# A two-layer gated transformer on one core: the router moved into attention layer 1, FFN normalisation into its second layer, a value projection split

## The chip, the cores and the metric

One core of a Trainium2 chip runs the whole program. The metric is the device time of one execution in microseconds; lower is better. An execution is the span that the profiler sees plus a little around it.

## What is computed

Cut to what matters (B=32 sequences, S=112 rows, D=256, 375 context rows, 16 heads of 16):

```
x = x + tanh(g_xattn[0]) * attention0(layernorm(x), ctx, mask0)
x = x + tanh(g_ffn[0])   * ffn0(layernorm(x))            # three +-1 weight matrices, 1024 wide
x = x + tanh(g_xattn[1]) * attention1(layernorm(x), ctx, mask1)
xf = layernorm(x)                                        # 3584 rows ("tokens")
probs = softmax(xf @ Wr)                                 # 8 experts
e = argmax(probs); rank = how many earlier tokens chose e; keep = rank < 448
y[token] = p[token] * relu(xf[token] @ W1[e]) @ W2[e]    for kept tokens
x = x + tanh(g_ffn[1]) * y
```

## The kernel before

Five engines run their own instruction lists and meet at semaphores. The phases run one after another, each in a block of its own: setup, queries 0, attention 0, FFN, queries 1, attention 1, logits, ranks, experts. Between two phases all engines meet and the semaphores of the old one are cleared.

`attention_phase` (L532) handles one sequence a step, software-pipelined and written out: in step s, `s.back(n)` is the sequence n steps older. Keys are made for s-1 (p), row maxima for s-3 (x), scores, exponentials and the weighted sum for s-4 (d), and the head outputs are turned, normalised, projected and added to the residual for s-5 (e). TensorE's `body` interleaves by hand 12 score units, 14 row scores, two key products, the value products (L770), the turns of e's heads (L833, L840), the projection (L856) and the weighted sum (L825). VectorE reduces each row score (L1030, "row") from a ring of three PSUM banks, splits keys (`low_keys`, L1069), normalises heads, and makes `low_heads` (L1061), which raises `back_ready`. ScalarE takes the exponentials (L952) and copies out of PSUM. GpSimd masks 8 of the 12 units (L699) and makes the low part of the context (L707). SyncE issues all loads and stores; `x_sum` (two buffers) is loaded at L674 and stored to DRAM at L681. After step 36 the phase ends.

`logits_phase` then reloads the rows from DRAM four sequences at a time, normalises them (with a square root on ScalarE), turns them and multiplies by Wr. `ranks_phase` is one chain of small VectorE instructions that makes expert, rank, slot and probability of every token. In `experts_phase` SyncE issues expert 0's weights (L1690, L1691), then waits for `put`, that is, for all 32 indirect DMAs (L1725) with which GpSimd scatters the rows to `expert_in`, and only then loads expert 0's rows. ScalarE and VectorE split the weights into high and low halves (L1784, L1824), TensorE turns the rows (L1740) and runs the products (L1757, L1771).

`ffn_phase` (L1112) takes four sequences a step. Its products are numbered z = 0 to 15: 0 to 7 are the first layer (4 matmuls each), 8 to 15 the second (16 each). VectorE makes the low half of each (L1233) and, for the next group, runs statistics after z=4 and the normalisation after z=6; TensorE turns those rows after z=11. Mask work stands at z=8, 9, 10, 14, 15.

## Time and profile before

| | |
|---|---|
| median of 3 runs | 1799.13 us (1794.83 to 1804.24) |
| profiled execution | 1798.14 us, of it span 1796.4 us |
| TensorE / VectorE / ScalarE / GpSimd busy | 84% / 62% / 45% / 47% |
| attention 1, last residual add to the experts' first product | 122.3 us |
| mean granted TensorE clock | 0.918 |

Busy shares are means over phases with different limits; the 122.3 us are from 1496.2 to 1618.46 in the profile. A clock of 1.00 is 2.4 GHz, 0.50 is 1.2 GHz.

### The profile page before, as it was taken

Reading aid. Unit: us, or ns where it says so; the run is one execution under the profiler, and the core shown is the slowest. Engines: PE = TensorE matmul, PEld = TensorE weight load, DVE = VectorE, ACT = ScalarE, POOL = GpSimd, SP = SyncE. Lnnn points to the kernel's source line nnn. Section 1 sums busy time; section 2 is a strip of 40 time slices with the busy share of each in tenths; the row PEclk is TensorE's granted clock in tenths of the full one; section 3 lists DMA queues with packets and bytes.
Section 4 is the critical chain, followed back from the end, with each engine's and each line's share of the span. In section 5 each row is a group of like instructions: output and inputs, shape, how many; then the busy total and the mean of one; then the engine's idle time right before and its main releaser. Section 6 shows DMA issues by size and latency. Waiting matters only on the chain. (4 is left out here: it accounts for less than half of the span.)

```text
span 1796.4 us, 41156 instructions
## 1 busy us (share of the span) xinstructions
PE 1502.7 (84%) x15399; PEld 1094.7 (61%) x15399; DVE 1113.2 (62%) x3561; ACT 802.7 (45%) x1822; POOL 846.8 (47%) x794
## 2 busy tenths in 40 slices
PE   1739999999996899999957379999999995509996
PEld 0417777777774466555634157777777774507775
DVE  4738788787783555555537267777777774515663
ACT  3316666666663222222203146666666652114441
POOL 1247787787774000000012447777777761064332
PEclk9869999999998899999978589999999996559998
DMA  7654455455431122221136545666566522035440
GB/s 230 217 107 97 97 112 104 98 115 101 97 80 34 42 64 69 83 69 58 33 87 206 106 103 122 125 119 114 113 122 125 108 47 69 26 120 171 135 148 18
DMA packets 225380, 183.65 MB, mean 102 GB/s; under 512 B 70314, under 2 KB 218735, under 8 KB 225192
## 3 DMA queue, kind: packets, MB, share of 16 engines
q1 hardware_dynamic: 219560, 171.36, 40.9%
q0 software_dynamic: 5632, 9.78, 1.7%
q8 instruction: 118, 1.93, 0.5%
q14 instruction: 70, 0.57, 0.1%
HBM read 99.53 MB, written 48.49 MB: 82 GB/s over the span
## 5 line engine op out<-in xcount | busy, mean ns | idle before, releaser
L952 ACT ACTIVATE probs_a<-bank 125x448 f32<-125x448 f32 x768 | 388.0, 541 | 32.9 <-PE bank L809 16.6
L699 POOL TENSOR_TENSOR probs_a<-probs_a,keep_a 125x448 int32<-125x448 int32 x256 | 285.3, 1137 | 121.4 <-ACT probs_a L952 121.3
L699 POOL TENSOR_TENSOR probs_a<-probs_a,mask_keep 125x448 int32<-125x448 int32 x256 | 285.3, 1137 | 99.2 <-ACT probs_a L952 99.0
L1030 DVE CUSTOM_DVE_ANT_0 masked_scores_a<-bank,mask_add_a 112x375 bf16<-112x375 f32 x512 | 260.7, 545 | 97.4 <-PE bank L780 93.6
L1030 DVE CUSTOM_DVE_ANT_0 masked_scores_a<-bank,mask_add 112x375 bf16<-112x375 f32 x512 | 260.3, 545 | 71.0 <-PE bank L780 67.4
L780 PE MATMUL bank<-k_stack_a,q_stack_a 96*128 96x375 f16 x1024 | 292.7, 327 | 8.1 <-DMA k_stack_a<-k_low_a 3.1
L809 PE MATMUL bank<-q_stack_a,k_stack_a 97*128 97x224 f16 x1536 | 253.1, 259 | 16.9 <-DMA q_stack_a<-max_t_a 16.1
L809 PEld LDWEIGHTS bank<-q_stack_a,k_stack_a 97*128 97x128 f16 x1536 | 146.0, 98 | 78.1 <-DMA q_stack_a<-max_t_a 18.0
L1354 PE MATMUL bank<-h0h_f,ffn_w 128*128 128x448 f16 x512 | 180.6, 353 | 11.6 <-DVE h0l_f L1233 11.4
L1354 PE MATMUL bank<-h0l_f,ffn_w 128*128 128x448 f16 x512 | 180.4, 352 | 0.0
L1193 POOL DMA_DIRECT2D x_after_ffn<-y_f x8 | 5.9, 743 | 346.1 <-DVE y_f L1240 346.1
L825 PE MATMUL bank<-probs_a,values_a 125*32 125x112 f32 x6144 | 161.7, 260 | 2.7 <-POOL probs_a L699 2.4
L825 PEld LDWEIGHTS bank<-probs_a,values_a 125*32 125x32 f32 x6144 | 144.8, 110 | 23.4 <-issue 19.3
L707 POOL TENSOR_TENSOR ctx_low_a<-ctx_in_a,ctx_high_a 128x375 f16<-128x375 f32 x128 | 113.0, 903 | 70.0 <-ACT ctx_high_a L930 70.0
L749 PE MATMUL bank<-ctx_high_a,wk_high 128*128 128x375 f16 x256 | 87.4, 341 | 51.5 <-POOL ctx_low_a L707 46.8
L975 ACT ACTIVATE heads_t_a<-bank 128x448 f32<-128x448 f32 x64 | 34.8, 544 | 204.5 <-PE bank L825 204.5
L780 PEld LDWEIGHTS bank<-k_stack_a,q_stack_a 96*128 96x128 f16 x1024 | 99.7, 98 | 43.4 <-DVE row_max_a L1030 10.9
L1305 ACT ACTIVATE h1h_f<-bank 128x448 f16<-128x448 f32 x64 | 34.8, 544 | 167.0 <-PE bank L1354 167.0
L1233 DVE SCALAR_TENSOR_TENSOR h1l_f<-bank,h1h_f 128x448 f16<-128x448 f32 x64 | 40.0, 625 | 111.0 <-ACT h1h_f L1305 111.0
L770 PE MATMUL bank<-wv_high,ctx_high_a 128*128 128x256 f16 x384 | 104.8, 273 | 1.7 <-DVE k_low_a L1069 1.6
L770 PE MATMUL bank<-wv_high,ctx_low_a 128*128 128x256 f16 x384 | 104.6, 272 | 0.0
L770 PE MATMUL bank<-wv_low,ctx_high_a 128*128 128x256 f16 x384 | 104.4, 272 | 0.0
(208 smaller groups left out, 3208.7 us busy)
## 6 DMA issues: line engine op xcount, KB each, us to landing
k_stack_a<-k_high_a SPq DMA_DIRECT2D x256, 96.0 KB, 4.1
ctx_in_a<-in_ctx_dram SPq DMA_DIRECT2D x64, 375.0 KB, 3.6
w_in_e<-in_L_ffn_W_dram SPq DMA_DIRECT2D x16, 1024.0 KB
k_stack_a<-k_low_a SPq DMA_DIRECT2D x128, 96.0 KB, 4.2
q_stack_a<-q_split SPq DMA_DIRECT2D x128, 84.0 KB, 3.4
x_and_bias<-xb_q SPq DMA_DIRECT2D x16, 448.0 KB, 4.5
q_split<-high_q SPq DMA_DIRECT2D x32, 224.0 KB, 3.7
x_sum_a<-x_and_bias SPq DMA_DIRECT2D x64, 112.0 KB, 4.2
```

The lines of the kernel that those rows point to most:

```text
L699: pool.tensor_tensor(bits, bits, cols, ALU.mult).then_inc(masked, 1)
L707: pool.tensor_tensor(ctx_low[s.four][:, cols], ctx_in[s.two][:, c, :], ctx_high[s.four][:, cols], ALU.subtract).then_inc(ctx_low_ready, 1)
L749: last = pe.matmul(work_bank[:, 0:S2], w[:, c, j * P:(j + 1) * P], part[p.four][:, c * S2:(c + 1) * S2], start=c == 0 and n == 0, stop=c = ...
L770: last = pe.matmul(work_bank[:, (k % 2) * D:(k % 2 + 1) * D], part[x.four][:, at:at + P], w[:, c, :], start=c == 0 and n == 0, stop=c == K ...
L780: pe.matmul(bank_of(x, h)[:, 0:S2], q_stack[x.four][0:STACK, at:at + P], k_stack[x.four][0:STACK, (h // 2) * WIDE:(h // 2) * WIDE + S2], s ...
L809: last = pe.matmul(bank[:, half * 2 * S:(half + 1) * 2 * S], k_stack[d.four][0:ROWS, at:at + P], q_stack[d.four][0:ROWS, (2 * t + half) * ...
L825: last = pe.matmul(head_bank[QUAD * j:QUAD * (j + 1), t * S:(t + 1) * S], values[d.two][:, k, 4 * t + j, :], probs[:, i, j * S:(j + 1) * S ...
L952: act.activation(probs[:, i, :], score_bank[i % 3][0:CK, 0:GT], ACT.Exp, scale=DK ** -0.5).then_inc(exped, 1)
L975: act.activation(heads_t[:, :], head_bank[:, 0:GT], ACT.Copy).then_inc(heads_ready, 1)
L1030: dve.tensor_tensor_reduce(masked_scores[:, use_of[x.value, h] % 3, :], bank_of(x, h)[0:S, 0:S2], mask_add[x.four][:, 0:S2], 1.0, -LARGEST ...
L1233: dve.scalar_tensor_tensor(out=low[:, j, :], in0=z_bank[z % 4][:, 0:GT], scalar=0.0, in1=high[:, j, :], op0=ALU.max, op1=ALU.subtract).the ...
L1354: last = pe.matmul(z_bank[z % 4][:, 0:GT], w[layer][:, c, j * P:(j + 1) * P], part[:, c, :], start=c == 0 and n == 0, stop=c == chunks - 1 ...
```

## The change

Logits and ranks phases go. Attention 1 gets their work, later in the pipeline: VectorE measures row f = s-6, GpSimd takes its power -0.5, ScalarE normalises row s-7 into `sent_rows`, TensorE turns it and in the next step multiplies it by Wr (`route_products`); four sequences together choose, count, order and place in the steps 12 to 15 behind their first, one or no small VectorE instruction in each of four slots of a step, and GpSimd scatters sequence s-16. The phase runs 48 steps in place of 37 (`LAG`). `x_sum` has four buffers. `make_values(0, 1)` is split in two calls in both layers. In the FFN, statistics move from z=4 to z=9, the end of normalisation from 6 to 11, the turn from 11 to 12, the low rows from 12 to 13, the mask's turn from 13 to 14.

```diff
-        attention_phase(nc, m, 1, based, out, a["ctx_1024"], (add_1, keep_1), q_split)
-        moe_phases(nc, m, a, expert_in, out)
+        attention_phase(nc, m, 1, based, out, a["ctx_1024"], (add_1, keep_1), q_split, (a["L1_ffn_Wr"], expert_in))
+        experts_phase(nc, m, a, expert_in, out)
...
-        x_sum = many(2, sb, "x_sum", [S, D], F32)
+        x_sum = many(4, sb, "x_sum", [S, D], F32)
...
+        LAG = 16 if layer else 5
...
-                    wait(sp, x_stored[d.two], 16 * d.use2)
-                    sp.dma_start(x_sum[d.two][:, :], take(x_in, d.value)).then_inc(x_loaded[d.two], 16)
+                    wait(sp, x_stored[d.four], 16 * d.use4)
+                    if layer:
+                        wait(sp, xn_ready, d.value - 3)
+                    sp.dma_start(x_sum[d.four][:, :], take(x_in, d.value)).then_inc(x_loaded[d.four], 16)
...
+            if layer:
+                sp.dma_start(wr[:, :, :], router.rearrange("(c p) e -> p c e", p=P)).then_inc(wr_loaded, 16)
...
-            run_quads(B, 5, body)
-            for n in range(2):
-                sp.wait_ge(x_stored[n], 16 * B // 2)
+            run_quads(B, LAG, body)
+            for n in range(4):
+                sp.wait_ge(x_stored[n], 16 * B // 4)
...
+            def take_root(f):
+                pool.wait_ge(measured, 4 * f.value + 3)
+                wait(pool, xn_ready, f.value)
+                pool.tensor_tensor(root[:, :], spread[:, :], half[:, :], ALU.pow).then_inc(rooted, 1)
+            def number_tokens(quad):
+                pool.wait_ge(routed, routed_at(quad, "shifted"))
+                slots = slice(G * (quad % 3), G * (quad % 3) + G)
...
+            def send_rows(w):
+                pool.wait_ge(routed, routed_at(w.quad, "put"))
+                pool.wait_ge(numbered, w.quad + 1)
...
+                at = G * (w.quad % 3) + w.four
+                pool.indirect_dma_start(expert_in[:, :],
+                                        bass.IndirectOffsetOnAxis(put[w.quad % 3][:, w.four:w.four + 1], 0),
+                                        sent_rows[:, at, :], None, bounds_check=E * CAP - 1,
+                                        oob_is_err=False).then_inc(sent[at], 16)
...
+                f = s.back(6)
                 for i in pool_units:
+                    if i == pool_units[5] and layer and f.exists(B):
+                        take_root(f)
...
+                if layer:
+                    t, w = s.back(14), s.back(16)
+                    if t.exists(B) and t.four == 0:
+                        number_tokens(t.quad)
+                    if w.exists(B):
+                        send_rows(w)
+            run_quads(B, LAG, body)
+            if layer:
+                for n in range(3 * G):
+                    pool.wait_ge(sent[n], 16 * len(range(n, B, 3 * G)))
...
-                elif p.exists(B):
+                elif ks[0] == 2 and p.exists(B):
                     pe.wait_ge(k_low_ready, KC * (p.value + 1))
-                else:
+                elif ks[0] == 2:
...
-                last.then_inc(v_made, 1)
+                if ks[-1] > 0:
+                    last.then_inc(v_made, 1)
+            def route_products(s, e):
+                f, r, t = s.back(7), s.back(8), s.back(12)
+                counts = t.exists(B) and t.four == 1
+                if not (f.exists(B) or r.exists(B) or counts):
+                    return
+                pe.wait_ge(back_ready, min(e.value + 1, B))
+                wait(pe, routes_kept, routes(s.value) - 1)
+                if r.exists(B):
+                    if r.value == 0:
+                        pe.wait_ge(wr_loaded, 16)
+                    for c in range(KC):
+                        last = pe.matmul(head_bank[0:S, 256:256 + E], xt[r.two][:, c, :], wr[:, c, :],
+                                         start=c == 0, stop=c == KC - 1)
...
+                    dst = head_bank[0:S, 288:288 + G * E].rearrange("s (b e) -> s b e", b=G)
+                    pe.matmul(dst, before[:, :], chosen[:, :, :], start=True, stop=False, skip_group_check=True)
+                    for b in range(1, G):
+                        pe.matmul(dst[:, b:, :], ones[:, :], chosen[:, b - 1, :].unsqueeze(1).to_broadcast([S, G - b, E]),
+                                  start=False, stop=False, skip_group_check=True)
+                    last = pe.matmul(dst, ones[:, :], carried[:, :].unsqueeze(1).to_broadcast([S, G, E]),
+                                     start=False, stop=True, skip_group_check=True)
+                if f.exists(B):
+                    pe.wait_ge(xn_ready, f.value + 1)
+                    for c in range(KC):
+                        last = pe.transpose(head_bank[:, c * S:(c + 1) * S],
+                                            sent_rows[:, f.value % (3 * G), c * P:(c + 1) * P], ident[0:S, 0:S])
+                last.then_inc(routes_made, 1)
...
+                if layer:
+                    wait(pe, routes_kept, routes(d.value + 4))
...
-                    make_values(x, p, e, (0, 1))
+                    make_values(x, p, e, (0,))
+                if layer:
+                    route_products(s, e)
+                if x.exists(B):
+                    make_values(x, p, e, (1,))
...
+            def normalise_rows(f):
+                act.wait_ge(measured, 4 * (f.value + 1))
+                wait(act, sent[f.value % (3 * G)], 16 * (f.value // (3 * G)))
+                act.activation(sent_rows[:, f.value % (3 * G), 0:D], x_sum[f.four][:, :], ACT.Identity,
+                               bias=shift[:, 0:1], scale=root[:, 0:1]).then_inc(xn_ready, 1)
+            def power_up(quad):
+                act.wait_ge(routed, routed_at(quad, "shifted"))
...
+                act.activation(power[:, :, :], shifted[:, :, :], ACT.Exp).then_inc(powered, 1)
+            def keep_routes(s):
+                f, r, t = s.back(7), s.back(8), s.back(12)
+                counts = t.exists(B) and t.four == 1
+                if not (f.exists(B) or r.exists(B) or counts):
+                    return
+                act.wait_ge(routes_made, routes(s.value))
+                if r.exists(B):
+                    last = act.activation(logits[r.quad % 2][:, r.four, :], head_bank[0:S, 256:256 + E], ACT.Copy)
+                if counts:
+                    last = act.activation(ranks[:, :, :].rearrange("s b e -> s (b e)"), head_bank[0:S, 288:288 + G * E],
+                                          ACT.Copy)
+                if f.exists(B):
+                    last = act.activation(xt[f.two][:, :, :], head_bank[:, 0:KC * S].rearrange("p (c t) -> p c t", c=KC),
+                                          ACT.Copy)
+                last.then_inc(routes_kept, 1)
...
+                if layer and f.exists(B):
+                    normalise_rows(f)
+                if layer and t.exists(B) and t.four == 1:
+                    power_up(t.quad)
...
                 units(9)
+                if layer:
+                    keep_routes(s)
                 if x.exists(B):
                     copy_values(x, e, (0, 1))
...
+            def measure(f, part):
+                if part == 0:
+                    dve.wait_ge(summed, f.value + 1)
+                    dve.bn_stats(stats[:, :], x_sum[f.four][:, :]).then_inc(measured, 1)
+                    return
+                if part == 1:
+                    dve.wait_ge(measured, 4 * f.value + 1)
+                    dve.bn_aggr(mean_var[:, :], stats[:, :]).then_inc(measured, 1)
+                if part == 2:
+                    dve.wait_ge(measured, 4 * f.value + 2)
+                    wait(dve, rooted, f.value)
+                    dve.tensor_scalar(spread[:, :], mean_var[:, 1:2], EPS, None, ALU.add).then_inc(measured, 1)
+                if part == 3:
+                    dve.wait_ge(rooted, f.value + 1)
+                    wait(dve, xn_ready, f.value)
+                    dve.tensor_scalar(shift[:, :], mean_var[:, 0:1], root[:, 0:1], -1.0, ALU.mult,
+                                      ALU.mult).then_inc(measured, 1)
+            def wide(table):
+                return table[:, :].unsqueeze(2).to_broadcast([S, G, E])
+            def choose(quad, part):
+                if part == 0:
+                    dve.wait_ge(routes_kept, routes(G * quad + 11))
+                    dve.tensor_reduce(top[:, :], logits[quad % 2][:, :, :], AX.X, ALU.max).then_inc(routed, 1)
+                if part == 1:
+                    dve.wait_ge(routed, routed_at(quad, "top"))
+                    wait(dve, powered, quad)
+                    dve.tensor_tensor(shifted[:, :, :], logits[quad % 2][:, :, :], wide(top), ALU.subtract).then_inc(routed, 1)
+                if part == 2:
+                    dve.wait_ge(routed, routed_at(quad, "shifted"))
+                    dve.scalar_tensor_tensor(out=marked[:, :, :], in0=shifted[:, :, :], scalar=0.0, in1=number[:, :, :],
+                                             op0=ALU.is_equal, op1=ALU.mult).then_inc(routed, 1)
+                if part == 3:
+                    dve.wait_ge(routed, routed_at(quad, "marked"))
+                    dve.tensor_reduce(first[:, :], marked[:, :, :], AX.X, ALU.min).then_inc(routed, 1)
+            def count(quad, part):
+                if part == 0:
+                    dve.wait_ge(routed, routed_at(quad, "first"))
+                    wait(dve, routes_made, routes(G * quad + 9) if quad else 0)
+                    dve.tensor_tensor(chosen[:, :, :], number[:, :, :], wide(first), ALU.is_equal).then_inc(routed, 1)
...
+            def order(quad, part):
+                if part == 0:
+                    dve.wait_ge(routed, routed_at(quad, "inverse"))
+                    slots = slice(G * (quad % 3), G * (quad % 3) + G)
+                    dve.tensor_scalar(sent_rows[:, slots, D], chance[:, :], m["gate"][0:S, 3:4], W_SCALE ** -2,
+                                      ALU.mult, ALU.mult).then_inc(routed, 1)
+                if part == 1:
+                    dve.wait_ge(routes_kept, routes(G * quad + 13))
+                    dve.tensor_tensor(carried[:, :], carried[:, :], counted[:, :], ALU.add).then_inc(routed, 1)
+                if part == 2:
+                    dve.tensor_tensor(picked[:, :, :], ranks[:, :, :], chosen[:, :, :], ALU.mult).then_inc(routed, 1)
...
+            def place_rows(quad, part):
+                if part == 0:
+                    dve.wait_ge(routed, routed_at(quad, "rank"))
+                    dve.tensor_scalar(over[:, :], rank[:, :], float(CAP), float(2 * E * CAP), ALU.is_ge,
+                                      ALU.mult).then_inc(routed, 1)
...
+            def route(t, part):
+                if layer and t.exists(B):
+                    (choose, count, order, place_rows)[t.four](t.quad, part)
...
+                rows(2)
+                if layer and o.exists(B):
+                    measure(o, 3)
+                rows(3)
+                rows_measured(0)
                 if p.exists(B):
                     low_keys(p, 0)
-                rows(4, 5, 6, 7)
+                rows(4)
+                rows_measured(1)
+                rows(5)
+                rows_measured(2)
+                rows(6, 7)
                 if p.exists(B):
                     low_keys(p, 1)
                 if e.exists(B):
                     normalise(e)
                 if x.exists(B):
                     shift_parts(x, 0)
-                rows(8, 9, 10)
+                rows(8)
+                route(t, 0)
+                rows(9)
+                route(t, 1)
+                rows(10)
+                route(t, 2)
                 if e.exists(B):
                     low_heads(e)
-                rows(11, 12)
+                rows(11)
+                route(t, 3)
...
-                        if z == 4:
+                        if z == 9:
                             normalise(s)
-                        if z == 6:
+                        if z == 11:
                             normalise_end(s)
-                        if z == 12:
+                        if z == 13:
...
-                        if z == 5:
+                        if z == 10:
                             act.wait_ge(var_ready, s.value + 1)
                             act.activation(dev[:, :], mean_var[:, :, 1], ACT.Sqrt, bias=m["eps"][0:S, :]).then_inc(dev_ready, 1)
-                        if z == 12:
+                        if z == 13:
                             for c in range(KC):
...
-                    if s.exists(NG) and z == 11:
+                    if s.exists(NG) and z == 12:
                         turn(s)
-                    if p.exists(NG) and z == 13:
+                    if p.exists(NG) and z == 14:
                         turn_mask(s, p)
                 if p.exists(NG):
...
-def moe_phases(nc, m, a, expert_in, out):
...
-def logits_phase(nc, m, a, x_in, route):
...
-def ranks_phase(nc, m, route):
...
-def experts_phase(nc, m, a, route, expert_in, out):
+def experts_phase(nc, m, a, expert_in, out):
...
-                    if isinstance(s.value, int) and s.value == 0:
-                        sp.wait_ge(put, 16 * B)
...
-            pool.wait_ge(m["experts_cleared"], 16)
-            for b in range(B):
-                pool.indirect_dma_start(expert_in[:, :], bass.IndirectOffsetOnAxis(route["put"][:, b:b + 1], 0),
-                                        route["rows"][:, b, :], None, bounds_check=E * CAP - 1,
-                                        oob_is_err=False).then_inc(put, 16)
```

## Rows read from the trace of the kernel before

**Rows 1.** Busy time by stretch: us, PE, PEld, DVE, ACT, POOL, PEclk, DMA, GB/s.
```profile
580.00:925.00 345.00, 314.98 (x1952) 193.22 (x1952) 171.44 (x352) 78.66 (x153) 5.95 (x8) 0.97 0.21 61
...
1200.00:1350.00 150.00, 144.76 (x1940) 114.38 (x1933) 113.13 (x423) 97.48 (x236) 112.13 (x106) 1.00 0.61 118
...
1569.50:1618.50 49.00, 1.79 (x9) 1.48 (x10) 8.06 (x12) 5.36 (x10) 32.31 (x34) 0.50 0.38 127
```
**Rows 2.** Chain that ended last: start us, us, what.
```profile
1570.49 40.96 issue
...
1618.46 11.57 PE bank L1757 x48
```
**Rows 3.** Timeline around the last two phases (start us, us, engine, line).
```profile
1495.77 0.43 DVE L1055 SCALAR_TENSOR_TENSOR x_sum_a<-bank,x_sum_a 112x256 f32<-112x256 f32 x1 [1.62 <-PE bank L856]
...
1501.96 0.40 SPq L1438 DMA_DIRECT2D wr_l<-in_L_ffn_Wr_dram  x1
...
1566.77 0.18 DVE L1619 TENSOR_SCALAR base_k<-first_k 112x32 f32<-112x32 f32 x1
...
1569.59 0.38 SPq L1690 DMA_DIRECT2D w_in_e<-in_L_ffn_W_dram  x1
...
1578.75 4.27 ACT L1784 ACTIVATE w_high_e<-w_in_e 128x512 f16<-128x512 f32 x8 [21.00 <-DMA w_in_e<-in_L_ffn_W_dram]
1579.41 4.99 DVE L1824 SCALAR_TENSOR_TENSOR w_low_e<-w_in_e,w_high_e 128x512 f16<-128x512 f32 x8 [7.54 <-issue]
```
**Rows 4.** Timeline, GpSimd: the last of the 32 scatters.
```profile
1609.25 0.94 POOL L1725 DMA_INDIRECT expert_in<-rows_r,put_r  x1 [0.30 <-issue]
```
**Rows 5.** TensorE's waits in the FFN (total us, times, longest).
```profile
PE bank L1354 <- DVE h0l_f L1233: 11.4, 9, 1.6
```
**Rows 6.** Timeline, VectorE, one FFN group.
```profile
680.54 1.41 DVE L1204 BATCH_NORM_STATS2 stats_f<-xg_f 112x6 f32<-112x256 f32 x4
682.09 0.38 DVE L1208 BATCH_NORM_AGGREGATE mean_var_f<-stats_f 112x2 f32<-112x6 f32 x4
...
684.01 1.38 DVE L1218 TENSOR_SCALAR xn_f<-xg_f,mean_var_f,scale_f 112x256 f32<-112x256 f32 x4
```
**Rows 7.** Timeline, TensorE, one step of attention 1.
```profile
1293.38 0.36 PE L840 MATMUL bank<-ident,heads_q_a 112*128 112x112 f32 x2
...
1294.58 0.27 PE L770 MATMUL bank<-wv_high,ctx_high_a 128*128 128x256 f16 x1
...
1295.24 0.32 PE L780 MATMUL bank<-k_stack_a,q_stack_a 96*128 96x375 f16 x1
```
**Rows 8.** Timeline, VectorE, the same step.
```profile
1288.76 0.55 DVE L1069 SCALAR_TENSOR_TENSOR k_low_a<-bank,k_high_a 128x375 f16<-128x375 f32 x1
...
1294.40 0.39 DVE L1061 TENSOR_TENSOR heads_low_a<-bank,heads_high_a 128x224 f16<-128x224 f32 x1 [0.23 <-ACT heads_high_a L996]
```
**Rows 9.** Timeline, GpSimd, the same step and the start of the next.
```profile
1292.80 3.32 POOL L699 TENSOR_TENSOR probs_a<-probs_a,keep_a 125x448 int32<-125x448 int32 x3 [0.30 <-ACT probs_a L952]
...
1297.64 1.76 POOL L707 TENSOR_TENSOR ctx_low_a<-ctx_in_a,ctx_high_a 128x375 f16<-128x375 f32 x2
1301.54 1.13 POOL L699 TENSOR_TENSOR probs_a<-probs_a,keep_a 125x448 int32<-125x448 int32 x1 [2.14 <-ACT probs_a L952]
```
**Rows 10.** Timeline: VectorE instructions beside GpSimd ones, two places.
```profile
930.41 4.63 POOL L351 TENSOR_TENSOR xb_q<-xg_q,bo 112x1024 f32<-112x1024 f32 x2 [11.06 <-DMA xg_q<-x_after_ffn]
...
932.77 2.29 DVE L383 TENSOR_TENSOR scale_q<-scale_q,seen 112x4 f32<-112x4 f32 x1
...
1469.12 7.71 POOL L699 TENSOR_TENSOR probs_a<-probs_a,keep_a 125x448 int32<-125x448 int32 x7 [3.69 <-ACT probs_a L952]
...
1472.43 1.14 DVE L1039 TENSOR_SCALAR max_parts_a<-row_max_a 112x8 f16<-112x8 f32 x1
```
**Rows 11.** Timeline: TensorE loads of the logits phase, and table loads of ScalarE.
```profile
1513.79 3.06 PEld L1460 LDWEIGHTS bank<-wr_l,xt_l 128*112 128x112 f32 x16 [1.77 <-ACT xt_l L1487]
...
1042.38 1.28 ACT L952 ACT_TABLE_LOAD   x1
```

296 lines of the change are left out of this document (86 added, 210 removed).

## The prediction

> **What bounds the kernel now.** I read the busy time by stretch first. In attention 1 TensorE is busy 144.76 of 150 us at full clock, and in the FFN 314.98 of 345 [rows 1]: there it sets the pace, and whatever is added to its list, or stalls it, costs time. VectorE and GpSimd are each at 112 to 113 of 150 us in attention 1, so they have 3.3 us idle in a step of about 13.5. Between the last residual add and the experts TensorE does little: from 1569.5 to 1618.5 it is busy 1.79 of 49 us, at clock 0.50 [rows 1]. The chain of waits says why: 40.96 us in which SyncE waits for the scatters, then a load, and the first expert product at 1618.46 [rows 2]. The timeline gives the other end: the last residual add ends at 1495.77 + 0.43 = 1496.20 [rows 3]. So 122.3 us lie between attention and experts, and that is what most of the change is about.
>
> **The stretch behind attention, after.** Five terms.
> (a) From the last add to GpSimd's root: statistics 0.35 (a quarter of 1.41 [rows 6]), their aggregate 0.1 (0.38 / 4), one small instruction 0.2 [rows 3], then the power. No row shows a power on GpSimd; I take 0.5, between 0.2 (a small VectorE instruction) and 2.35 (half of 4.63, GpSimd's 1024-wide addition [rows 10]). With the hops 1.5.
> (b) GpSimd's list then holds 11 scatters (sequences 21 to 31, one a step, in the steps 37 to 47). One takes 0.94 + 0.30 idle = 1.24 [rows 4]: 13.7. The chain that places the last four sequences (turn, logits, copy, some 15 small VectorE instructions of 0.2, the count products) is 8 to 9 us and runs beside the first seven scatters (8.7), so it sets nothing, or 1 us.
> (c) The last scatter's landing: before, the last one ended at 1609.25 + 0.94 = 1610.19 and SyncE went on at 1570.49 + 40.96 = 1611.45 [rows 2, 4]: 1.3.
> (d) Ending the block: before, 1496.20 to 1501.96 [rows 3] is 5.8 with the store of the last rows in it, which I estimate at half; 2.8 is left, and 26 more semaphores to clear, an estimated 0.04 each, make it 3.8.
> (e) From the experts' first weight load to their first product: no scatter is waited for, and rows of expert 0 are issued right behind its weights. Then the weight split is last: it ended at 1579.41 + 4.99 = 1584.40, 14.8 behind the load's issue at 1569.59 [rows 3]. The two low row halves of about 0.6 each come behind it: 16.1, against 48.9 before.
> Sum: 1.5 + 13.7 + 1.3 + 3.8 + 16.1 = 36.4. The stretch shrinks by 122.3 - 36.4 = **85.9 us**. The bounds are narrow, 80 to 89. If the rows of expert 0 queued behind expert 1's weights, they would land some 9 us later (the first weights landed at 1578.75, 9.2 behind their issue [rows 3]); the row load is issued ahead of them, so I don't count it.
>
> **FFN.** TensorE waited 11.4 us for the low halves of the first layer [rows 5]: statistics (1.41 + 0.38) and normalisation (1.38) stand between products of four matmuls [rows 6]. Behind z=9 and z=11 they stand between products of sixteen, 3 us each, where VectorE has only 0.6 us of its own besides the mask. The 11.4 go. What is late next: z=8 to 10 now carry mask work of 0.9 to 1.9 us and the statistics, so the normalised rows are ready about 0.25 us after TensorE asks for them behind z=12, in 7 groups: 1.8 back. Gain **9.6 us** (bounds 5 and 11.4).
>
> **Projection split.** In layer 0 the two calls follow each other with nothing between and no new wait; nothing. In layer 1 it only makes room for `route_products`, costed below. Four `x_sum` buffers: SyncE's new wait for the normalised row asks for one of the step before, already there; behind it in SyncE's queue are the key stores and the row maxima's DMA, which would pay if it were late. Router weights and small constants at the start: **1 us** (0 to 2).
>
> **The router inside attention 1.** This is the price. Per step, TensorE gets two fp32 turns and two logit products. At 1.2 GHz a pass took 3.06 / 16 = 0.19 [rows 11], so 0.1 at full clock: 0.4, and 0.45 with a quarter of the five count products. ScalarE gets an identity and two copies, about 0.9, and GpSimd a scatter of 1.24 behind the context work, where it has 2.14 us idle before the next step's first mask [rows 9], and the root. Neither should be late.
> VectorE decides. `route_products` waits for `low_heads` of the same step, before needed only by the projection, 1.8 us later. In the step shown, the value products of `make_values(0)` end at 1294.58 [rows 7], and `low_heads` ran 1294.40 to 1294.75, having waited 0.23 for ScalarE [rows 8]. Ahead of it VectorE now does statistics 0.35, aggregate 0.1 and two tiny ones 0.1 each overlapped; from step 12 three more small ones, 0.3. Without anything else `low_heads` ends at 1294.75 + 0.8 = 1295.55: TensorE stalls 1.0 and works 0.45, so 1.45 a step (1.15 without the three).
> But there is the second thing that the rows show. A VectorE instruction with two SBUF inputs, normally 0.16, took 2.29 when it began beside a GpSimd instruction and ended with it (932.77 + 2.29 = 935.06 against 930.41 + 4.63 = 935.04); a tiny SBUF-to-SBUF scalar instruction took 1.14, one GpSimd unit, at 1472.43 [rows 10]. Of the new small instructions, nine in four steps are of these kinds (two in choose, one in count, three in order, three in place). GpSimd is busy without a break from 1292.80 to 1296.12 [rows 9], just where their slots lie (behind rows 8, 9 and 10). Each can wait for the end of a unit of 1.1 us. Going through the step by hand, with GpSimd's units 0.3 later, `low_heads` ends near 1297.1 in choose, order and place and near 1295.8 in count; with the maxima's scalar instruction sometimes caught too, a step costs 3.0 on average, and 1.65 in the steps without them. Some will find a gap. I take 2.6, nearer the locked end since the rows show the lock twice, and 1.3 for the others. Steps 12 to 34 are 23: 59.8. Steps 7 to 11: 6.5. Draining steps: 2. Sum **68.3 us**; bounds 14 (TensorE's 0.45 in 30 steps alone) and 91 (3.4 each).
> The Trainium skill, SBUF — State Buffer, "SBUF: two separate sides", calls this an exclusive lock: VectorE in a two-port mode or with two SBUF inputs against GpSimd, the loser blocked for the whole instruction. By that rule, applied to every one of the nine, the price is the 80 of the locked case; by an average port share it would be the 41 of the free one. It speaks against the change.
> No table load is counted: attention 1 has its own at 1042.38, 1.28 us [rows 11], and copies stand between the exponentials without one, but no row has an identity beside them. The Trainium skill, ScalarE: Activation LUTs, "Table sets: the hidden batching unit", says that identity is in every set; no row here shows it for this one.
>
> **Sum.** 1798.14 - 85.9 - 9.6 + 1 + 68.3 = 1771.9 for the profiled execution, which lies 1.0 below the median of the runs: **1773 us**.
>
> **Rivals.**
> R1, VectorE's new work slips into its 3.3 us of idle time. For it: the idle time; GpSimd's units move too when TensorE is late. Against: the slots lie in its busiest part. At 1.45 and 1.15 a step the cost is 33 + 6 + 2 = 41, less where turns overlap, 35: 1740.
> R2, the lock bites everywhere: 80 us, 1784; with GpSimd's scatter also holding the small ones, 91, 1796.
> R3, slower: the root on GpSimd. Its list then sets the step: root, three units, context, scatter, mask. After the scatter it has 0.9 us before unit 0, and about 1.5 till its context work is needed. From a root of 2.7 us on, the change gains nothing beyond what is measurable; at 3.5 it costs 2.0 in 30 steps on top, 60: 1833. For it: no row has its price. Against: 1024 elements take 2.35.
> R4, identity and exponential change tables: two loads of 1.28 in 31 steps, 79: 1852. Against: the copies.
> R5, the change doesn't do what it says: the stall in the FFN only moves to the turn behind z=12, 9.6 back: 1782; inside my range.
>
> **How the numbers follow.** Forecast 0.50 (1752 to 1784), R1 0.25, R2 0.12, R3 0.06, R4 0.02, R5 0.05. The range, 1738 to 1797, takes in R1's centre and R2 and leaves out R3, R4 and the better half of R1. About 0.5%, 9 us, is what a measurement can tell from no change. Faster by more: forecast, R1, R5 and half of R2 and a little less, 0.86; same, the rest of R2, 0.06; slower 0.08.
>
> **What would show it.** Right: experts' first load some 20 us behind the last residual add, their first product 16 later; L1354's wait for VectorE gone; in attention 1 a wait of TensorE at the turns or logit products of 1 to 2.5 us a step, ended by `low_heads`; tiny VectorE instructions of 0.5 to 1.1 us ending with GpSimd units. Wrong: steps under 14.5 us (R1), GpSimd without idle time and TensorE waiting for masks or context (R3), table loads between exponentials (R4), or a wait elsewhere, as for the first key product behind the statistics placed ahead of `low_keys` (about 0.25 a step in my sum).

## The result, and the profile after

The changed kernel takes **1809.7 us** (median of 8 runs, 1804.75 to 1813.52) against 1799.47 of the kernel before on the same chip: ratio 1.0059, 95% interval 1.0039 to 1.0079. I forecast 1773 in a range of 1738 to 1797, so the change loses a little where I expected it to win. Its profiled execution spans 1811.9 us, against 1796.4 before. Where the 15.5 us between the spans lie, from the residual adds and the first expert product in both traces:

| stretch | before | after | difference | forecast |
|---|---|---|---|---|
| up to the first residual add of attention 1 | 1073.72 | 1061.77 | -12.0 | -8.6 |
| attention 1, first to last residual add | 422.1 | 534.8 | **+112.7** | +68.3 |
| end of the last add to the first expert product | 122.3 | 39.4 | -82.9 | -85.9 |
| the experts, first product to the end | 177.9 | 175.5 | -2.4 | 0 |

So both gains came, and the price in attention 1 is what I got wrong, by 44 us. The busy time by stretch (us, PE, PEld, DVE, ACT, POOL, PEclk, DMA, GB/s) answers to [rows 1]:
```profile
1200.00:1350.00 150.00, 131.32 (x1522) 99.87 (x1520) 109.03 (x376) 80.43 (x202) 95.35 (x96) 0.88 0.47 93
1350.00:1500.00 150.00, 130.12 (x1548) 99.69 (x1549) 111.75 (x391) 81.64 (x208) 97.28 (x98) 0.91 0.47 93
1500.00:1560.00 60.00, 53.09 (x676) 40.60 (x674) 42.44 (x153) 29.25 (x74) 36.81 (x37) 0.87 0.30 53
```
TensorE now idles 19 of 150 us where it idled 5, and the granted clock, which was 1.00 all through this stretch, is 0.88 and 0.91. No other engine has become full: in the first of these rows VectorE and GpSimd are less busy than before (109.03 and 95.35 us against 113.13 and 112.13). TensorE's longest list of waits (us in total, times, longest) has a new first line, and the FFN's line of [rows 5] is gone:
```profile
PE bank L863 <- DVE heads_low_a L1306: 57.1, 26, 3.2
...
PE bank L1753 <- DMA xg_e<-expert_in: 26.5, 1, 26.5
PE bank L1593 <- DVE xn_f L1486: 17.4, 2, 17.2
```
The timeline of one choose step (start us, us, engine, line, idle before) shows what is behind it:
```profile
1310.99 0.57 POOL L741 TENSOR_TENSOR root_a<-spread_a,half_a 112x1 f32<-112x1 f32 x1
...
1311.47 2.32 DVE L1214 SCALAR_TENSOR_TENSOR marked_a<-shifted_a,number_a 112x32 f32<-112x32 f32 x1
1311.54 2.20 POOL L736 TENSOR_TENSOR probs_a<-probs_a,keep_a 125x448 int32<-125x448 int32 x2
1313.72 0.38 DVE L1306 TENSOR_TENSOR heads_low_a<-bank,heads_high_a 128x224 f16<-128x224 f32 x1
...
1314.15 0.92 PE L863 MATMUL bank<-wr_a,xt_a 128*112 128x8 f32 x4 [2.52 <-DVE heads_low_a L1306]
```
`marked`, the third of the step's small VectorE instructions and the second that GpSimd holds up, begins 0.09 before GpSimd's root ends (1310.99 + 0.57 = 1311.56) and ends at 1313.79, just when both mask units behind the root have ended (1313.74). It works 0.19 us when nothing is in its way (run `e2_slots_first` below), so it waited through two units, not one. `heads_low` stands behind it, and TensorE stands 2.5 us at the logit products. What then happens to the clock, in stretches of 1.7 us:
```profile
1309.60:1311.30 1.70, 1.70 (x17) 1.41 (x15) 1.70 (x8) 1.70 (x6) 1.41 (x2) 1.00 0.82 170
1311.30:1313.00 1.70, 0.33 (x4) 0.05 (x1) 1.70 (x3) 0.39 (x1) 1.70 (x3) 1.00 1.15 127
1313.00:1314.70 1.70, 0.55 (x3) 0.55 (x4) 1.66 (x5) 0.00 (x0) 0.74 (x1) 0.74 0.68 85
1314.70:1316.40 1.70, 1.70 (x10) 1.36 (x11) 0.00 (x0) 0.42 (x2) 0.00 (x0) 0.50 0.30 50
...
1319.80:1321.50 1.70, 1.70 (x30) 1.07 (x32) 1.22 (x4) 0.00 (x0) 1.53 (x3) 0.75 0.02 5
```
TensorE is busy 0.88 of 3.4 us, and the clock falls from 2.4 to 1.2 GHz until about 1320.6; the products run at half speed for nearly 7 us, a loss of some 3.4 us on top of the wait. The wait comes back in each choose, order and place step, 17 times with 2.3 us or more, and the low clock stands behind 15 of the 17, for 88.7 us in all. From the residual adds most of these steps take 19 to 21 us, count steps 16, and the steps of the kernel before mostly 13.5 to 14.5. Two of the waits, 3.02 and 2.51 us, have no low clock behind them (the row from 1356 to 1392 has 1.00), and their steps took 17.5 and 17.0 us:
```profile
1356.00:1392.00 36.00, 30.46 (x448) 23.97 (x448) 29.56 (x102) 19.78 (x50) 24.97 (x26) 1.00 0.46 101
```
So in this trace the low clock makes such a step some 2.7 us longer than the wait alone.

### The profile page after: what moved, and what is told of

It reads as the page before. It is cut to its first block and busy times, and to the rows that moved or that the text cites. A ratio compares the mean times of both kernels' runs of the same rounds, so it can differ in the third digit from the quotient of the medians.

```text
span 1811.9 us, 41668 instructions
## 1 busy us (share of the span) xinstructions
PE 1534.3 (85%) x15435; PEld 1104.4 (61%) x15435; DVE 1155.5 (64%) x3677; ACT 821.2 (45%) x1907; POOL 865.4 (48%) x824
## 5 line engine op out<-in xcount | busy, mean ns | idle before, releaser
L1275 DVE CUSTOM_DVE_ANT_0 masked_scores_a<-bank,mask_add_a 112x375 bf16<-112x375 f32 x512 | 266.2, 542 | 132.8 <-PE bank L887 132.7
L887 PE MATMUL bank<-k_stack_a,q_stack_a 96*128 96x375 f16 x1024 | 304.1, 339 | 6.6 <-DVE row_max_a L1275 2.9
L916 PE MATMUL bank<-q_stack_a,k_stack_a 97*128 97x224 f16 x1536 | 259.6, 264 | 6.0 <-DMA q_stack_a<-max_t_a 5.1
L916 PEld LDWEIGHTS bank<-q_stack_a,k_stack_a 97*128 97x128 f16 x1536 | 149.7, 100 | 69.4 <-issue 6.6
L887 PEld LDWEIGHTS bank<-k_stack_a,q_stack_a 96*128 96x128 f16 x1024 | 103.5, 102 | 44.1 <-DVE row_max_a L1275 11.4
L846 PE MATMUL bank<-wv_high,ctx_high_a 128*128 128x256 f16 x384 | 108.8, 283 | 1.7 <-DVE k_low_a L1314 1.6
L846 PE MATMUL bank<-wv_high,ctx_low_a 128*128 128x256 f16 x384 | 108.8, 283 | 0.0
L846 PE MATMUL bank<-wv_low,ctx_high_a 128*128 128x256 f16 x384 | 108.5, 283 | 0.0
```

The source lines that it names most:

```text
L846: last = pe.matmul(work_bank[:, (k % 2) * D:(k % 2 + 1) * D], part[x.four][:, at:at + P], w[:, c, :], start=c == 0 and n == 0, stop=c == K ...
L887: pe.matmul(bank_of(x, h)[:, 0:S2], q_stack[x.four][0:STACK, at:at + P], k_stack[x.four][0:STACK, (h // 2) * WIDE:(h // 2) * WIDE + S2], s ...
L916: last = pe.matmul(bank[:, half * 2 * S:(half + 1) * 2 * S], k_stack[d.four][0:ROWS, at:at + P], q_stack[d.four][0:ROWS, (2 * t + half) * ...
L1275: dve.tensor_tensor_reduce(masked_scores[:, use_of[x.value, h] % 3, :], bank_of(x, h)[0:S, 0:S2], mask_add[x.four][:, 0:S2], 1.0, -LARGEST ...
```

## The experiments

In each run the kernel before ran on the same chip; ratios are to it, with the 95% interval. "Attention 1" is the time from the first to the last residual add (422.1 before, 534.8 after).

**`e1_late_products`: the router's products just ahead of the projection** (my first theory was that all that counts is TensorE's early wait for `low_heads`).
```diff
                     make_values(x, p, e, (0,))
-                if layer:
-                    route_products(s, e)
...
                 rows(13)
+                if layer:
+                    route_products(s, e)
                 if e.exists(B):
```
(ScalarE's `keep_routes` moves to the step's end with it.)

> The changed kernel with the router's products on TensorE moved from between the two value products to just ahead of the projection, and ScalarE's copies of them to the end of its step; VectorE's list is untouched, so its small instructions still stand beside GpSimd's units. Theory A (low_heads comes late because small VectorE instructions wait for GpSimd, and the early wait for it stalls TensorE, after which its clock falls): the wait of 57 us falls to under 20, the granted clock in attention 1 goes back above 0.97, and the time falls by 60 to 80 us to about 1740. Theory B (VectorE simply has too much work in the step, wherever TensorE waits): the wait only moves to the projection and to the row banks, the time falls by less than 20 us, to 1790 or more.

Measured: 1843.3 us, ratio 1.0251 (1.0226 to 1.0277); attention 1 took 567.2. A miss of 100 us, and the timeline tells how (one place step):
```profile
1297.11 0.57 POOL L741 TENSOR_TENSOR root_a<-spread_a,half_a 112x1 f32<-112x1 f32 x1
...
1297.56 5.12 DVE L1260 SCALAR_TENSOR_TENSOR place_a<-first_a,rank_a 112x4 f32<-112x4 f32 x1
1297.66 3.30 POOL L736 TENSOR_TENSOR probs_a<-probs_a,keep_a 125x448 int32<-125x448 int32 x3
1300.93 1.73 POOL L766 TENSOR_TENSOR ctx_low_a<-ctx_in_a,ctx_high_a 128x375 f16<-128x375 f32 x2
```
GpSimd's work now follows the root without a gap: five instructions, three mask units and two of the context, and `place` ends with the last of them (1302.68 against 1302.66). Of the wait at the logit products (L863) 1.3 us were left, and TensorE stood at the row scores (L887) and at the turn of the row maxima (L896) instead, up to 4.7 us at a time:
```profile
PE bank L887 <- DVE row_max_a L1275: 48.1, 20, 4.5
PE bank L896 <- DVE row_max_a L1275: 34.2, 22, 4.7
```
This points at VectorE's instruction, wherever TensorE meets it; e2 and e14 below test it.

**`e2_slots_first` and `e3_both`: the first three VectorE slots at the step's start.** The latter has e1's late products too.
```diff
+                route(t, 0)
+                route(t, 1)
+                if t.four != 1:
+                    route(t, 2)
                 rows(2)
...
-                rows(8)
-                route(t, 0)
-                rows(9)
-                route(t, 1)
-                rows(10)
-                route(t, 2)
+                rows(8, 9, 10)
+                if t.four == 1:
+                    route(t, 2)
```

> The changed kernel with the router's small VectorE instructions of slots 0, 1 and 2 moved from behind rows 8, 9 and 10 to the start of the step, ahead of row 2, where VectorE waits for TensorE and GpSimd has few units (the third slot of the counting step stays, as it needs the powers of the same step). The products stay where the change has them. Theory A (the lock with GpSimd is what delays low_heads): the instructions shrink from 0.5 to 2.3 us to about 0.2, a step costs about 1.5 us over before as in the unlocked case, and the time is 1745 to 1765, the upper end if the clock still falls. Theory B (amount of work on VectorE): the same instructions cost the same in total, the time stays above 1790.

> Both moves together. Theory A: nothing waits for low_heads any more, TensorE has only its added 0.45 us a step, the clock stays at 1.00: attention 1 costs 14 to 25 us over before, the time is 1715 to 1730. Theory B: above 1780.

Measured: e2 1727.8 us, ratio 0.9612 (0.9587 to 0.9637), attention 1 450.8, better than expected; e3 1719.5 us, ratio 0.9551 (0.9524 to 0.9578), 445.1, as expected. The same instructions, in e2, by line (count | busy us, mean ns), and its wait at the logit products:
```profile
L1214 DVE SCALAR_TENSOR_TENSOR marked_a<-shifted_a,number_a 112x32 f32<-112x32 f32 x8 | 1.5, 193 | 0.3
...
L1260 DVE SCALAR_TENSOR_TENSOR place_a<-first_a,rank_a 112x4 f32<-112x4 f32 x8 | 1.2, 151 | 0.0
```
```profile
PE bank L863 <- DVE heads_low_a L1306: 3.5, 10, 1.0
```
0.19 and 0.15 us instead of 2.3, 3.5 us of waiting instead of 57, and the clock is 1.00 again. The late products, beside which e1 got slower, bring another 0.6% here.

**`e4_ffn_alone`: the kernel before with only the FFN's new places** (`normalise` at z=9 instead of 4, its end at 11 instead of 6, and what follows from them).
```diff
-                        if z == 4:
+                        if z == 9:
                             normalise(s)
...
-                        if z == 6:
+                        if z == 11:
                             normalise_end(s)
```

> The kernel before with the FFN's part of the change alone (statistics behind z=9, normalisation behind 11, turn behind 12, low rows behind 13, mask's turn behind 14). As predicted: 9.6 us faster than before, so about 1789. Rival (the stall moves to the turn): within 2 us of before.

Measured: 1785.1 us, ratio 0.9914 (0.9885 to 0.9942). The traces say 12.1 us: the load that starts attention 1's queries lies at 913.70 instead of 925.75. TensorE's wait for `h0l_f`, 11.4 us, is gone and none came in its place. From the last residual add of attention 0 to that load, which leaves out what came before, it is 338.1 us instead of 351.8, so 13.6 less (11.1 less in the changed kernel).

**`e5_fill_stall`: the changed kernel, TensorE kept working in the stall.** 24 useless products ahead of the wait for `low_heads`, in steps 12 to 34 but for count.
```diff
+            wv_fill = m["wv"][layer][0]
...
+                if 12 <= s.value < 35 and t.four != 1:
+                    for _ in range(24):
+                        pe.matmul(work_bank[:, 256:448], wv_fill[:, 0, 0:P], wv_fill[:, 1, 0:192], start=True, stop=True, skip_group_check=True)
                 pe.wait_ge(back_ready, min(e.value + 1, B))
```

> The changed kernel with 24 useless f16 matmuls of 192 columns (0.08 us each at full clock, 1.9 us) on TensorE just ahead of its wait for low_heads, in steps 12 to 34 except the counting ones, where it otherwise stands idle for 2.5 to 3.2 us. Nothing else is changed, so VectorE's waits for GpSimd stay. Theory C (a part of the loss is TensorE's clock, which falls to half behind each such stall): the half-clock stretches in attention 1, 88 us in the changed kernel, fall to under 30, and the time falls by 20 to 40 us, to 1770 to 1790. Theory D (the clock is a by-product; VectorE's list alone sets the step): the time stays within 8 us of 1810.

Measured: 1777.3 us, ratio 0.9888 (0.9857 to 0.9918), 32 us less than the changed kernel (31 by the ratios) for more work; attention 1 498.0, 36.8 less. By stretch, the clock is back:
```profile
1200.00:1350.00 150.00, 140.88 (x1847) 111.32 (x1839) 122.53 (x421) 84.52 (x223) 106.05 (x108) 1.00 0.53 104
```
VectorE's instructions are untouched (`marked` still takes 2.3 us), and the useless products take up part of the wait (25.0 us of it are left) without ending it sooner. Of the 88.7 us at the low clock, 3.4 are left. So the run parts the two: the low clock after the stall costs some 32 to 37 of the 112.7 us.

**`e6_early_wait`: the kernel before with only the split and the early wait.**
```diff
-                last.then_inc(v_made, 1)
+                if ks[-1] > 0:
+                    last.then_inc(v_made, 1)
...
                 if x.exists(B):
-                    make_values(x, p, e, (0, 1))
+                    make_values(x, p, e, (0,))
+                if layer and e.exists(B):
+                    pe.wait_ge(back_ready, e.value + 1)
+                if x.exists(B):
+                    make_values(x, p, e, (1,))
```

> The kernel before with the projection split and, between its halves in attention 1, only the wait for low_heads of the same step, without any router work. By the rows of before TensorE gets there at 1294.58 and low_heads ends at 1294.75, so 0.2 us a step, some 5 us: 1800 to 1808. If the early wait by itself were the cause (its place, not what delays low_heads), it would cost over 20 us.

Measured: 1801.7 us, ratio 1.0021 (1.0006 to 1.0036): about 4 us, as expected. The wait asked 1.8 us earlier is nearly free by itself: what counts is what delays `low_heads`.

**`e7_small_two_source` and `e9_small_one_source`: the kernel before with three useless small VectorE instructions** behind rows 8, 9 and 10 in steps 12 to 35, an addition of two [112 x 32] tiles in e7, of one tile and a constant in e9.
```diff
+            def small(s, n):
+                if layer and 12 <= s.value < 36:
+                    dve.tensor_tensor(scr[n][:, :], scr_a[:, :], scr_b[:, :], ALU.add).then_inc(small_done, 1)
...
-                rows(8, 9, 10)
+                rows(8)
+                small(s, 0)
+                rows(9)
+                small(s, 1)
+                rows(10)
+                small(s, 2)
```

> The kernel before with one useless VectorE addition of two [112, 32] SBUF tensors behind each of the rows 8, 9 and 10 in steps 12 to 35 of attention 1 (72 instructions of 0.19 us); no router, no early wait. Theory W (an instruction with two SBUF inputs waits until GpSimd has nothing ready, so for its whole run of units): single instructions of 3 to 5 us, 2 to 4 us a step and more where the clock follows, the time is 1850 to 1930. Theory U (it waits for the one unit that runs, as I predicted): none above 1.15 us, the time is 1805 to 1835.

> The same as e7 with instructions of one SBUF input (the same tensor plus a constant). If the wait for one unit belongs to this kind, as the maxima's scalar instruction of 1.14 us in before suggests, none is above 1.15 us and the time is 1805 to 1835, well under e7. If the kind makes no difference, it equals e7.

Measured: 1817.4 us, ratio 1.0111 (1.0081 to 1.0141), and 1816.2 us, 1.0115 (1.0083 to 1.0147). 72 instructions take 756 and 757 ns in the mean and none over 1.18 us, so one source or two is the same. In e7's timeline:
```profile
1300.24 3.32 POOL L701 TENSOR_TENSOR probs_a<-probs_a,keep_a 125x448 int32<-125x448 int32 x3 [0.30 <-ACT probs_a L954]
1300.60 0.83 DVE L1042 TENSOR_TENSOR scr_a<-scr_a_a,scr_b_a 112x32 f32<-112x32 f32 x1
1301.81 0.71 DVE L1042 TENSOR_TENSOR scr_a<-scr_a_a,scr_b_a 112x32 f32<-112x32 f32 x1
```
Three units of 1.11 us from 1300.24 end at 1301.35, 1302.45 and 1303.56; the two additions end at 1301.43 and 1302.52, each with one unit. This is what I had forecast of the lock. Most steps take 14.8 us, attention 1 takes 441.9, 19.8 more than before, and the clock stays at 1.00. The lock by single units isn't what made steps of 20 us.

**`e10_root_last`: the changed kernel, only GpSimd's root moved** from between the masks to behind the context work.
```diff
                 for i in pool_units:
-                    if i == pool_units[5] and layer and f.exists(B):
-                        take_root(f)
...
                     low_context(s, 1)
+                if layer and f.exists(B):
+                    take_root(f)
```

> The changed kernel with one thing moved: GpSimd takes its power (the root, 0.57 us) behind the context work, at the end of its step, in place of between units 6 and 7. VectorE's small instructions and TensorE's early wait stay where the change has them. In the changed kernel the long waits (2.3 us, and 5.1 with the products late) are all of a two-input instruction that arrives 0.1 us before the root ends, and last through all units behind it; the others last to the end of one unit. Theory R (the root, or an arrival beside it, is what makes the long wait): no instruction above 1.2 us, the time falls by 25 to 50 us to 1760 to 1785. Theory S (any second locked instruction in a step waits for the run): still over 2 us in each such step, the time stays within 10 us of 1810.

Measured: 1757.2 us, ratio 0.9822 (0.9791 to 0.9853); attention 1 478.7. In a choose step:
```profile
1220.12 3.32 POOL L736 TENSOR_TENSOR probs_a<-probs_a,keep_a 125x448 int32<-125x448 int32 x3 [0.67 <-ACT probs_a L1065]
1221.70 0.70 DVE L1214 SCALAR_TENSOR_TENSOR marked_a<-shifted_a,number_a 112x32 f32<-112x32 f32 x1
1222.32 0.38 DVE L1306 TENSOR_TENSOR heads_low_a<-bank,heads_high_a 128x224 f16<-128x224 f32 x1
```
```profile
PE bank L863 <- DVE heads_low_a L1306: 35.5, 26, 2.1
```
`marked` takes 0.70 instead of 2.32 and ends at 1222.40, with the second unit (1220.12 + 2.21 = 1222.33). TensorE waits 35.5 us instead of 57.1, never over 2.1, and the clock is 0.99 where it was 0.88. One instruction of 0.57 us in another place is worth 2.4%, some 42 us, within the fall that I had expected. (The two traces differ by 56.1 us in attention 1: the changed kernel's is of its slowest run, e10's of its fastest.)

**`e11_small_beside_power` and `e12_small_beside_add`: e7 and a useless [112 x 1] instruction on GpSimd at the root's place**, a power in e11, an addition in e12.
```diff
...
+                    if i == pool_units[5] and layer and 12 <= s.value < 36:
+                        pool.tensor_tensor(gp_c[:, :], gp_a[:, :], gp_b[:, :], ALU.pow).then_inc(gp_done, 1)
                     if d.exists(B):
                         mask_unit(d, i)
```

> Kernel e7 (before, with three useless two-input VectorE additions a step) and a useless power of a [112, 1] tensor on GpSimd between units 6 and 7, in steps 12 to 35. In e7 the additions waited 0.7 to 0.83 us, to the end of one unit. Theory R: the second addition, which will arrive beside the power, now lasts 2 us or more in most steps, and the time rises by over 20 us above e7's 1817. Theory S: waits stay at 0.7 to 1.1 us, the time rises by the 0.57 us at most, to under 1830.

> The same with an addition in place of the power on GpSimd, so a short instruction at the same place. If the long wait comes from the power itself, it is absent here; if from where VectorE's instruction arrives beside any short instruction ahead of a run, it may be here too, and the time is that of e11 or between e7 and e11.

Measured: e11 1889.0 us, ratio 1.0548 (1.0510 to 1.0587); e12 1866.3 us, ratio 1.0421 (1.0385 to 1.0457). So 24 instructions of 0.55 us on an engine with idle time cost 4.4% beyond e7, some 78 us, and 24 of 0.19 us cost 3.1%. First e11, then e12:
```profile
1292.32 0.55 POOL L717 TENSOR_TENSOR gp_c_a<-gp_a_a,gp_b_a 112x1 f32<-112x1 f32 x1
1292.80 2.30 DVE L1047 TENSOR_TENSOR scr_a<-scr_a_a,scr_b_a 112x32 f32<-112x32 f32 x1
1292.84 3.30 POOL L702 TENSOR_TENSOR probs_a<-probs_a,keep_a 125x448 int32<-125x448 int32 x3
```
```profile
1303.45 0.19 POOL L717 TENSOR_TENSOR gp_c_a<-gp_a_a,gp_b_a 112x1 f32<-112x1 f32 x1
1303.60 2.23 POOL L702 TENSOR_TENSOR probs_a<-probs_a,keep_a 125x448 int32<-125x448 int32 x2
1303.93 1.94 DVE L1047 TENSOR_TENSOR scr_a<-scr_a_a,scr_b_a 112x32 f32<-112x32 f32 x1
```
e11 makes the long wait from parts, in the kernel before: the addition ends at 1295.10, two units behind the power (1292.84 + 2.20 = 1295.04). A third unit and the context work follow without a gap, so here the wait ends inside the run, where in e1 it ended with it. e12 says that it isn't the power as an operation: a plain addition of 0.19 does it too, though the VectorE instruction comes 0.3 us into the unit behind it (it ends at 1305.87, with the second unit, 1305.83). The clock from 1200 to 1350 is 0.91 and 0.95 in these two and 1.00 in e7, though no stall of TensorE in e12 is long; the longest line of its waits there is
```profile
PE bank L794 <- DVE row_max_a L1039: 30.8, 23, 1.5
```

**`e14_late_root_last` and `e13_all_three`: e1 and e3, each with e10's edit.**

> e1_late_products and e10_root_last together: the router's products just ahead of the projection, GpSimd's root behind its context work, the VectorE instructions still behind rows 8, 9 and 10. Theory R (e1 lost because the second small VectorE instruction met the root and waited through five GpSimd units, 5.1 us, where in the changed kernel it was 2.3): the 5.1 us instructions are gone, none is longer than 1.2 us, steps are 15 to 16.5 us, and since the products have 2 us more room than in e10 it comes out at or below e10, 1735 to 1757. Rival L (late products are themselves what cost e1 its 34 us against the changed kernel, by holding ScalarE's or VectorE's work for the next step): it stays above e10 by 20 us or more, 1780 to 1830, with short VectorE instructions and a wait elsewhere.

> e3_both with GpSimd's root behind its context work as well. Theory R: with the first three VectorE slots at the step's start nothing small lies beside the root or the run of masks behind it any more, so moving the root brings nothing: within 5 us of e3_both, 1714 to 1725. Rival: the root in the middle of the masks costs the masks or the small instructions left behind rows 2 to 7 something still; then 1700 to 1713. If the root now comes too late for the scatter in the same step, a few us more than e3_both, 1726 to 1735.

Measured: e14 1730.4 us, ratio 0.9629 (0.9613 to 0.9645), attention 1 454.9. The one edit that parts it from e1 takes away 6.2% of the kernel before's time, some 112 us, and e1's miss is settled: late products are good, the root ahead of GpSimd's run is what hurt. TensorE's wait at the turn of the row maxima, 34.2 us and up to 4.7 at a time in e1, is small:
```profile
PE bank L896 <- DVE row_max_a L1275: 15.1, 22, 1.1
```
e13 1713.3 us, ratio 0.9530 (0.9513 to 0.9548), attention 1 433.8. That is 0.2% under e3, with intervals that overlap, so I can't say that the root still costs something there. With e3 it is the fastest version, 4.7% under the kernel before: the change's idea was sound, and its order within the step was not. Over the kernel before, attention 1 grew, in one trace of each, by 145.1 us in e1, 112.7 in the changed kernel, 76.0 in e5, 56.7 in e10, 32.8 in e14, 28.7 in e2, 23.1 in e3 and 11.7 in e13.

## Why the prediction was wrong, point by point

**The stretch behind attention: right.** Forecast 36.4, measured 39.4. The chain and the timeline, which answer to [rows 2 to 4]:
```profile
1621.41 0.40 SPq L1712
...
1621.86 7.70 DMA w_in_e<-in_L_ffn_W_dram
...
1630.24 4.90 DVE w_low_e L1837 x8
1635.14 1.07 DVE x_low_e L1862 x2
1636.22 0.14 issue
1636.35 11.77 PE bank L1770 x48
```
```profile
1596.56 0.42 DVE L1300 SCALAR_TENSOR_TENSOR x_sum_a<-bank,x_sum_a 112x256 f32<-112x256 f32 x1 [2.66 <-PE bank L965]
...
1597.94 0.57 POOL L741 TENSOR_TENSOR root_a<-spread_a,half_a 112x1 f32<-112x1 f32 x1 [4.45 <-DVE spread_a L1193]
...
1611.32 0.94 POOL L755 DMA_INDIRECT expert_in<-sent_rows_a,put_a  x1 [0.30 <-issue]
```
(a) The root ends 1.5 behind the last add (1598.51 against 1596.98), as forecast; it takes 0.57 where I took 0.5. (b) Eleven scatters end at 1612.26, 13.75 later; forecast 13.7. (c) and (d) The first load comes 9.15 behind that, where I had 5.1. The lines of the block's end say where the 4 us are (ns: shortest, median, longest; start of the first and the last):
```profile
L1376 POOLq DRAIN  x2: 2673/3455/4237, 564.5 to 1614.1; - x2
L97 SPq EVENT_SEMAPHORE_RANGE_CLEAR  x72: 25/30/35, 1617.0 to 1621.1; - x72
```
GpSimd drains for 2.67 us from 1614.11; only then do the engines meet and SyncE clears the 72 semaphores, 4.1 us. Before, the same drain began at 1486.0, beside attention's last work, and clearing 46 semaphores took 3.1 us. So the 26 more cost the 1.0 us that I had estimated; what I had at nothing is the drain, which now stands behind the last scatter, and some 1 us is the rest of (d) and the landing, which I had a little short. (e) 14.9 from the load to the first product, forecast 16.1, with the weight split last, as said. It makes up for 1.2 of the 4, by luck.

**FFN: right in kind, too low.** 12.1 to 13.6 by e4 against 9.6, above my bound of 11.4. The stall went as said; the 1.8 us that I took back at the turn didn't come, no wait is left there. What comes on top of the 11.4 us of waiting isn't traced.

**Projection split, start: nothing speaks against it.** The first residual add is 12.0 earlier, the FFN's 12.1. But kernels that don't differ up to that add (before, e7, e9, e11, e12) have it anywhere from 1067.85 to 1074.92, so the 1 us that I had for the start can't be read.

**The router in attention 1: the failed step**, 112.7 against 68.3, and above the bound of 91. The place of the wait was right (TensorE at the logit products, ended by `low_heads`), and so were the instructions that delay it and the lock that delays them. Wrong was the sentence "each can wait for the end of a unit of 1.1 us". Some waited longer: behind the root, for two units in the changed kernel (2.3 us) and five instructions in e1 (5.1 us). With the root elsewhere (e10) each waits for one unit, and attention 1 grows by 56.7 us, inside my bounds and below my 68.3. So the term was sized rightly for single units, with bounds that had no room for the run, and 56 of the 112.7 us in the traces (42 by the medians of the runs) hang on the root's place. This share and that of the clock below overlap: with the root elsewhere TensorE's wait falls by 21.6 us, and most of the low clock goes with it. I had the root in view, but only asked how long it takes (R3), not what lies behind it when it ends.

The second omission is in the sum itself, which has **no term for the clock**. [rows 1] showed 1.00 in this stretch, and I carried it over to a kernel into which I had just put a stall. Roughly, the 112.7 are 57.1 of waiting, some 40 of lost clock (0.12 x 150, 0.09 x 150, 0.13 x 60, and 3 from 1060 to 1200, at 0.98) and 14 of the work added to TensorE (my 0.45 in 31 steps); this split is an estimate, and e5 shows 32 to 37 of the 40. The Trainium skill, TensorE: Matmul & The Clock Gate, "HAM oscillation — how this bites in real kernels", describes a wait that comes back with every tile and leaves TensorE at its low clock each time; the trace agrees in the main, with 0.50 granted behind 15 of the 17 long stalls, for nearly 7 us behind eleven of them.

**Rivals.** R1 (idle time absorbs it, 35 us) is out for this order, but in e13's order the router costs less still: 11.7 us in attention 1, about TensorE's added work alone. R2 (lock everywhere) had the right side and priced a lock of one unit; 1796 was its end. (Its 91 us can't be had from 3.4 us in 23 steps: with 1.65 in five and 2 for draining that is 88.5. Nothing hangs on it.) R3: the root takes 0.57, not 2.7, and GpSimd isn't full; a slow root isn't it. R4: no table load lies between the exponentials, though an identity ran at 1308.36 between exponentials in the step shown; the Trainium skill, ScalarE: Activation LUTs, "Table sets: the hidden batching unit", had it so, and the trace agrees. R5 fell with e4.

**The chances.** I gave 0.08 to a slower kernel and all of it to R3 and R4, two prices of single instructions. The slower case that came about was in the mechanism on which the forecast itself stood, and I gave no chance to its price being more than one unit.

## What to carry over

Before small VectorE instructions are put into a step, look at what GpSimd does at their slots: the price is not their 0.15 us but the end of GpSimd's unit, and, where a short GpSimd instruction stands ahead of back-to-back work, the end of the second unit behind it or of a later one, up to the fifth. Put them where GpSimd idles, and short GpSimd instructions behind its long ones. A wait that is new on TensorE is to be priced with the clock that follows it, and where two small edits interact (late products: 1.9% slower with the root between the masks, 2.0% faster without), neither can be judged alone.

## What the runs showed of the hardware

- VectorE beside GpSimd: 72 small SBUF instructions of some 0.15 to 0.19 us took 756 ns (two sources) and 757 ns (one source) in the mean. The Trainium skill, SBUF — State Buffer, "SBUF: two separate sides", has the loser of the shared port pair blocked for a whole instruction; e7 agrees, with both additions ending with a unit. That a VectorE instruction stays blocked through two or five GpSimd instructions in a row (2.30 and 5.12 us) is more than that rule says.
- Some VectorE instructions were not held up beside a GpSimd unit. In the changed kernel `spread` (L1193, one source, [112 x 1]) began inside a unit in 28 of 32 steps and took 0.15 us each time, and the reduction `top` (L1207, [112 x 32] to [112 x 4]) did in six of eight and took 0.18. No run here shows why.
- What stays open is the rule by which VectorE misses the boundary between two GpSimd units, and how many it misses. It happened behind a short GpSimd instruction, power or addition: in e11 the second slot took 2.30 to 2.35 us in 21 of 24 steps and 3.39 in two, in e12 1.93 to 1.94 us in 20 of 24, 0.84 in three and 1.17 in the last.
- GpSimd's power on [112 x 1] takes 0.57 us, its addition 0.19.
- The length of one stall doesn't tell whether TensorE's clock falls. It stood at 0.99 with stalls of up to 2.1 us in some steps (e10, with four short falls) and fell to 0.50 behind 15 of 17 stalls of 2.3 to 3.2 us in the changed kernel; but in e12, with no stall over 1.9 us, it fell 13 times. Which property decides was not tried.
